# A fused token, attention and mixture-of-experts layer: the attention's normalisation on whole tiles of patches and of text

## The reference

```python
h = tok(x)                      # layernorm over 768, @ W (768x256) + bias, layernorm over 256, + position; class token first
h = concat([h, txt], axis=1)    # (16, 69, 256)
h = h + attn(layernorm(h))      # q, k, v = x @ w.T; rotary embedding; softmax(q k / 16) v, per image
h = h + ffn(layernorm(h))       # shared expert + 2 of 8 routed experts (256 -> 1024 -> 256, gelu) + x
```

## Time and profile before

| | |
|---|---|
| median of three runs | 359.08 us |
| the profiled execution, its own time | 360.22 us |
| its span, first to last instruction | 358.4 us |
| mean granted TensorE clock | 0.952 |
| TensorE busy | 309.5 us (86%) |
| GpSimd busy | 203.3 us (57%) |
| VectorE busy | 160.0 us (45%) |
| ScalarE busy | 152.5 us (43%) |

### The profile page before, as it was taken

How to read it: one execution, slowest core, us unless ns; L and a number is a source line. 1 busy time by engine, 2 the same in 40 slices (tenths; PEclk the granted TensorE clock), 3 DMA queues, 4 the chain that set the end, 5 groups by cost and what they waited for, 6 DMA issues and landing times.

```text
span 358.4 us, 6664 instructions
## 1 busy us (share of the span) xinstructions
PE 309.5 (86%) x2063; PEld 275.4 (77%) x2064; DVE 160.0 (45%) x398; ACT 152.5 (43%) x327; POOL 203.3 (57%) x155
## 2 busy tenths in 40 slices
PE   1778387899857897999989999999999999999970
PEld 1556246898737697899968998998998998998970
DVE  3244656888835264966414332332332332332320
ACT  2364431457676582435234433433433433434310
POOL 1242110843866300046598889889988889535651
PEclk9969769899985999999999999999999999999998
DMA  7934101031345433016635336523455433333522
GB/s 253 284 119 156 33 15 38 2 117 37 87 136 182 140 98 103 2 59 215 227 112 190 118 136 190 175 89 116 161 146 161 142 49 59 44 44 44 59 31 29
DMA packets 21357, 39.39 MB, mean 110 GB/s; under 512 B 2855, under 2 KB 17658, under 8 KB 19034
## 3 DMA queue, kind: packets, MB, share of 16 engines
q0 software_dynamic: 7392, 25.43, 26.5%
q1 hardware_dynamic: 13658, 13.51, 12.0%
q10 hardware_dynamic: 288, 0.20, 0.2%
HBM read 28.32 MB, written 6.93 MB: 98 GB/s over the span
## 4 chain that ended last, share of the span: by engine, by line
PE 42%; POOL 13%; DVE 12%; issue 12%; DMA 11%; ACT 3%; POOLq 3%; SPq 1%; DVEq 0%
DMA out_tokens<-xy_all,dest 10%; PE ps L898 8%; PE ps L900 8%; PE ps L899 8%; PE ps L949 7%; POOL ring L397 6%; PE ps L777 5%; PE ps L805 3%; POOL ring L396 3%; POOL out_tokens L517 2%; POOLq L514 2%; PE ps L869 2%; DVE h L1186 1%; PE ps L1012 1%; DVE st L1194 1%
## 5 line engine op out<-in xcount | busy, mean ns | idle before, releaser
L397 POOL TENSOR_TENSOR ring<-stage,ring 128x512 fp32r<-128x512 f32 (+2 forms) x30 | 76.1, 2536 | 2.5
L1439 DVE TENSOR_TENSOR hgT<-ps,hgT 128x512 fp32r<-128x512 f32 x50 | 32.2, 686 | 72.3 <-ACT hgT L767 72.3
L898 PE MATMUL ps<-ring,hgT 128*128 x200 | 58.0, 290 | 2.1 <-DVE xy_all L1445 1.5
L900 PE MATMUL ps<-ring,hgT 128*128 x200 | 55.9, 279 | 0.0
L899 PE MATMUL ps<-ring,hgT 128*128 x200 | 55.9, 279 | 0.0
L517 POOL DMA_INDIRECT out_tokens<-xy_all,dest x25 | 39.5, 1581 | 27.6 <-DMA out_tokens<-xy_all,dest 15.4
L759 ACT ACTIVATE hg<-ps 128x512 f32<-128x512 f32 x50 | 29.9, 599 | 47.7 <-PE ps L900 47.7
L507 POOL DMA_INDIRECT xy_all<-normalized_tokens,dest x25 | 24.9, 995 | 43.0 <-DVE dest L1401 35.7
L898 PE MATMUL ps<-ring,xgT 128*128 x100 | 41.3, 413 | 1.1 <-issue 0.6
L396 POOL TENSOR_SCALAR ring<-stage 128x512 fp32r<-128x512 f32 (+2 forms) x30 | 38.5, 1283 | 2.7 <-PEq L1026 2.5
L898 PEld LDWEIGHTS ps<-ring,hgT 128*128 128x128 f32 x200 | 37.6, 188 | 2.6 <-issue 2.6
(11 more groups left out here) (182 smaller groups left out, 602.2 us busy)
## 6 DMA issues: line engine op xcount, KB each, us to landing
stage<-in_w_up POOLq DMA_DIRECT2D x9, 1024.0 KB, 5.4
stage<-in_w_dn POOLq DMA_DIRECT2D x9, 1024.0 KB, 5.5
xg<-xy_all SPq DMA_DIRECT2D x25, 128.0 KB, 2.0
xp<-in_patches SPq DMA_DIRECT2D x4, 384.0 KB, 5.4
normalized_tokens<-hn SPq DMA_DIRECT2D x4, 276.0 KB
residual_tokens<-h SPq DMA_DIRECT2D x4, 276.0 KB
ring<-in_tok_w SPq DMA_DIRECT2D x1, 768.0 KB, 6.1
base<-residual_tokens SPq DMA_DIRECT2D x2, 384.0 KB, 3.6
```

The source lines that it names most:

```text
L397: return nc.gpsimd.tensor_tensor(lo, stage[:, part, c0:c1], hi.bitcast(F32), ALU.subtract)
L898: nc.tensor.matmul(o, a[0], b[0], start=n == 0, stop=False)
L900: last = nc.tensor.matmul(o, a[1], b[0], start=False, stop=n == len(pairs) - 1)
L1439: v.tensor_tensor(hgT[:, c, 1, 4 * half:4 * half + 4, :], ps[:, turned_bank + half, :].rearrange("p (k t) -> p k t", k=4), hgT[:, c, 0, 4 ...
```

## The change

1. The attention's first normalisation is made on tiles as they lie: on the five patch tiles in `tt` (which gets five buffers) and on four tiles of text rows (`xtxt`, 4 images x 32 rows each, loaded from HBM on its own). The class token is one more row (row 64) of the short tile. `attention_front`, `attention_bias`, `attention_norm` are per tile `i`, no longer per group `g`, and no longer read `h`.
2. Each of the nine tiles is transposed with two transposes. The copies out of PSUM (high on ScalarE, low on VectorE) put the columns where each image's sequence wants them, directly in `hT_n` (`placings`): one instruction for a text tile, two or three for a patch tile, since a tile cuts through images.
3. The DMAs from `tt` to `h` stay, but `h` is now first read by `attention_end`.
4. The short patch tile comes first. The text's normalisation and the high part of wq, wk, wv go to GpSimd, the position table gets `ln2_b` tile by tile, and the sum for the class token is part of `tok_end(0)`. The orders of all engines up to the first scores are rewritten.
5. `attention_qk(g)` waits for the last tile of its group (`LAST_TILE` = 1, 2, 3, 4 for the four groups).

```diff
+SHORT = NB * NPATCH % P
+TROWS = [SHORT] + [P] * (NB * NPATCH // P)
+NPT = len(TROWS)
+FIRST = [sum(TROWS[:i]) for i in range(NPT)]
...
+        def runs_of(i):
+            runs = []
+            for b, first, row, n in parts_of(i):
+                if runs and n == NPATCH and runs[-1][4] == NPATCH:
+                    runs[-1][1] += 1
+                else:
+                    runs.append([b, 1, first, row, n])
+            return runs
...
+        LAST_TILE = [max(i for i in range(NPT) if FIRST[i] < GB * NPATCH * (g + 1)) for g in range(NG)]
...
+        def placings(k, n):
+            src = turned_tile(k)
+            if k < NG:
+                return [(columns(n, GB * k, GB, 1 + NPATCH, SEQ), src.rearrange("p c (b s) -> p c b s", s=NTXT))]
+            pairs = []
+            for b, images, first, row, rows in runs_of(k - NG):
+                pairs.append((columns(n, b, images, 1 + first, 1 + first + rows),
+                              src[:, :, row:row + images * rows].rearrange("p c (b s) -> p c b s", s=rows)))
+            if k == NG:
+                pairs.append((columns(n, 0, NB, 0, 1), src[:, :, SHORT:SHORT + 1].unsqueeze(2).to_broadcast([P, KD, NB, 1])))
+            return pairs
...
+            sp.dma_start(xtxt[:, :, :], txt.rearrange("(g b) s d -> (b s) g d", g=NG)).then_inc(rows_of_text_in, 16)
             for n, v in enumerate((ln2_g, ln2_b)):
                 sp.dma_start(vecs[:, n, :], v.partition_broadcast(P)).then_inc(tok_vec_in, 16)
+            load_places(0)
             load_patches(3, NPT)
...
+            sp.dma_start(h[0:1, :, :], tt[SHORT:SHORT + 1, 0:1, :].to_broadcast([1, NB, D])).then_inc(text_in, 16)
...
+            pool.dma_start(tt[SHORT:SHORT + 1, 0, :], cls_token).then_inc(cls_in, 16)
+            pool.dma_start(pe[SHORT:SHORT + 1, 0, :], cls_pos).then_inc(cls_in, 16)
+            nc.gpsimd.memset(trs[:, :], 1.0).then_inc(ones_ready, 1)
...
+            def text_norm():
+                pool.wait_ge(x_stats, 1)
+                root(xrs[:, :], xmv[:, :, 1], P, x_rstd)
+                pool.wait_ge(x_rstd, 1)
+                for j in range(NG):
+                    nc.gpsimd.tensor_scalar(xtxt[:, j, :], xtxt[:, j, :], xmv[:, j, 0:1], xrs[:, j:j + 1], ALU.subtract,
+                                            ALU.mult).then_inc(x_normed, 1)
+
+            def place_rows_of(i):
+                pool.wait_ge(pe_in[i], 16 * (1 if i == 0 else 2))
+                r = TROWS[i]
+                nc.gpsimd.tensor_tensor(pe[0:r, i, :], pe[0:r, i, :], vecs[0:r, 1, :], ALU.add).then_inc(pe_ready, 1)
+
+            def attention_weights():
+                pool.wait_ge(attn_w_in, 48)
+                nc.gpsimd.tensor_scalar(wqk2[:, 0, :, :, :].rearrange("p w k d -> p (w k d)"),
+                                        wqk[:, :, :, :].rearrange("p w k d -> p (w k d)"), 1.0, 0.0, ALU.mult, ALU.add)
+                nc.gpsimd.tensor_scalar(wv2[:, 0, :, :].rearrange("p k d -> p (k d)"),
+                                        wvs[:, :, :].rearrange("p k d -> p (k d)"), 1.0, 0.0, ALU.mult, ALU.add).then_inc(a_whi, 1)
 
...
-            pool.wait_ge(pe_in, 16 * 9)
-            nc.gpsimd.tensor_tensor(pe[:, 0:NPT - 1, :], pe[:, 0:NPT - 1, :],
-                                    vecs[:, 1, :].unsqueeze(1).to_broadcast([P, NPT - 1, D]), ALU.add)
-            n = TROWS[NPT - 1]
-            nc.gpsimd.tensor_tensor(pe[0:n, NPT - 1, :], pe[0:n, NPT - 1, :], vecs[0:n, 1, :], ALU.add).then_inc(pe_ready, 1)
+            place_rows_of(0)
             tok_root2(0)
-            tok_root(3)
+            tok_root(4)
             load_weights(0)
+            attention_root(0)
+            place_rows_of(1)
             tok_root2(1)
-            tok_root(4)
+            attention_root(1)
+            attention_weights()
+            place_rows_of(2)
+            tok_root2(2)
             load_weights(1)
-            tok_root2(2)
-            attention_root(0)
+            attention_root(2)
+            place_rows_of(3)
             tok_root2(3)
-            attention_root(1)
+            attention_root(3)
+            place_rows_of(4)
             tok_root2(4)
+            attention_root(4)
             pool.wait_ge(a_w, 1)
             pool.wait_ge(t_mm, NPT)
-            attention_root(2)
+            pool.wait_ge(t_done, NPT)
             piece(0, 0)
             piece(0, 1)
-            attention_root(3)
...
+            def attention_copy(k):
+                act.wait_ge(a_tr, k + 1)
+                for o, i in placings(k, 0):
+                    last = nc.scalar.activation(o, i, ACT.Copy)
+                last.then_inc(a_hT, 1)
...
+            tok_turned(1)
+            tok_norm(2)
+            tok_norm(3)
+            tok_turned(2)
+            attention_copy(0)
+            attention_copy(1)
+            tok_norm(4)
             attention_norm(0)
-            tok_turned(NPT - 1)
-            attention_copy(0)
+            tok_turned(3)
+            attention_copy(2)
+            attention_copy(3)
+            attention_copy(4)
...
+            def attention_transposes(k):
+                if k < NG:
+                    te.wait_ge(x_normed, k + 1)
+                    rows = xtxt[:, k, :]
+                else:
+                    te.wait_ge(a_normed, k - NG + 1)
+                    rows = tn[0:AROWS[k - NG], k - NG, :]
+                if k >= 2:
+                    te.wait_ge(a_low, k - 1)
+                r = rows.shape[0]
+                for c in range(KD):
+                    last = transpose(turned_tile(k)[:, c, 0:r], rows[:, P * c:P * (c + 1)], r)
                 last.then_inc(a_tr, 1)
 
             def attention_qk(g):
-                te.wait_ge(a_low, g + 1)
+                te.wait_ge(a_low, NG + LAST_TILE[g] + 1)
                 if g == 0:
                     te.wait_ge(a_w, 1)
+                    te.wait_ge(t_aff, NPT)
...
+            tok_transposes(1)
+            tok_product(0)
+            tok_transposes(2)
+            attention_transposes(0)
+            attention_transposes(1)
+            tok_product(1)
+            tok_transposes(3)
+            attention_transposes(2)
+            attention_transposes(3)
+            tok_product(2)
+            attention_transposes(4)
+            tok_transposes(4)
+            tok_product(3)
+            attention_transposes(5)
+            tok_product(4)
+            attention_transposes(6)
             attention_qk(0)
...
+                r, n = AROWS[i], NPT + i
+                v.scalar_tensor_tensor(out=tt[0:r, i, :], in0=tt[0:r, i, :], scalar=trs[0:r, n:n + 1], in1=pe[0:r, i, :],
                                        op0=ALU.mult, op1=ALU.add).then_inc(t_done, 1)
...
+            def attention_front(i):
+                dve.wait_ge(t_done, i + 1)
+                r = AROWS[i]
+                link(v.bn_stats(ast[0:r, i, :], tt[0:r, i, :]))
+                link(v.bn_aggr(amv[0:r, i, :], ast[0:r, i, :]))
+                v.tensor_scalar(amv[0:r, i, 1:2], amv[0:r, i, 1:2], EPS, None, ALU.add).then_inc(a_stats, 1)
+
+            def attention_bias(i):
+                dve.wait_ge(a_rstd, i + 1)
+                r = AROWS[i]
+                v.scalar_tensor_tensor(out=anb[0:r, i:i + 1], in0=amv[0:r, i, 0:1], scalar=-1.0, in1=ars[0:r, i:i + 1],
+                                       op0=ALU.mult, op1=ALU.mult).then_inc(a_norm_in, 1)
...
+            def attention_low(k):
+                dve.wait_ge(a_hT, k + 1)
+                for (o, i), (high, _) in zip(placings(k, 1), placings(k, 0)):
+                    last = v.tensor_tensor(o, i, high.bitcast(F32), ALU.subtract)
+                last.then_inc(a_low, 1)
...
                 dve.wait_ge(a_pv, g + 1)
+                if g == 0:
+                    dve.wait_ge(text_in, 32)
+                for i in range(LAST_TILE[g - 1] + 1 if g else 0, LAST_TILE[g] + 1):
+                    dve.wait_ge(img_in[i], 16 * len(parts_of(i)))
...
+            text_stats()
+            tok_stats(3)
+            tok_shift(3)
+            tok_stats2(0)
+            tok_stats(4)
+            tok_end(0)
+            attention_front(0)
+            tok_shift(4)
+            attention_low(0)
+            attention_low(1)
+            attention_bias(0)
+            tok_stats2(1)
+            tok_end(1)
+            attention_front(1)
+            attention_low(2)
+            attention_low(3)
+            attention_bias(1)
             tok_stats2(2)
-            attention_front(0)
+            attention_weights()
+            attention_low(4)
             tok_end(2)
-            attention_bias(0)
-            attention_weights()
+            attention_front(2)
+            attention_bias(2)
             tok_stats2(3)
-            attention_front(1)
+            attention_low(5)
             tok_end(3)
-            attention_bias(1)
-            attention_low(0)
+            attention_front(3)
+            attention_bias(3)
             tok_stats2(4)
+            attention_low(6)
             tok_end(4)
```

(6 more changed lines are left out.)

200 lines of the change are left out of this document (75 added, 125 removed).

## The result

The changed kernel takes 348.69 us (median of 4 runs, 346.34 to 352.28) against 359.08: ratio 0.967, 95% interval 0.956 to 0.978. Predicted were 345.0 us and 341 to 351.5. Run again on another chip, beside 17 runs of the kernel before (median 359.28, 355.4 to 361.7), it took 349.22 us (6 runs, 347.55 to 352.62), ratio 0.976, interval 0.970 to 0.983. So it is faster by 2 to 4%, some 10 us (the second interval alone reaches down to 1.7%).

What follows compares the result with a forecast made beforehand. Start-stage stops at the class token and the DMAs into `h` were taken to bound the kernel; terms up to the probabilities summed to 14.1 us off 359.08, giving 345.0 us, with 341 to 351.5 for 8 in 10.

Steps and rivals of the forecast that it cites:

- What bounds it, and that the gain goes through: Start stages: stops at the class token's sum and 4.49 us of DMA issue into `h`; gains there move all that follows.
- To the end of the fourth tile's bias: Token stage's start: third tile's bias, text statistics, GpSimd's root and text normalisations, fourth tile's root and bias, ending at 17.4.
- GpSimd's form with two columns: Four text normalisations 128x256 on GpSimd with two columns as operands: 0.5 us each, 2.0 in all, ends 1.2 and 2.6.
- The tiles: ScalarE's turn (8.6 us), then VectorE's turns per tile, until `attention_qk(0)` starts at 41.0 in place of 52.28.
- rival 2: Small placed instructions, GpSimd's forms and contention all at upper ends: 5.6 us more, 350.5 us; chance 0.14.
- Contention: Work moved to GpSimd can stop VectorE before `attention_qk(0)`: 1.7 us taken, ends 0 and 4.3.
- the estimate by that rule: Waits for the port pair shared by GpSimd and VectorE: two of 0.3 to 0.6 and one of 1.2, 2.0 us.
- The clock ahead of the scores: `attention_qk(0)` to first scores: half clock for 3.1 us loses 1.55; 10.15 us in all, scores at 51.1.
- Scores to the shared expert: Attention loop: clock loss not paid again, shorter way to probabilities, fewer transposes; lead grows from 10.4 to 14.1 us.
- the 0.55: Net gain per group, taken twice, from groups 0 and 1 losing their eight transposes from TensorE's queue.
- From there the same distance as before: From the shared expert's first product, expected near 83, to the end: orders and distance unchanged, no more gain counted.
- Rival 1: TensorE stays at half clock in the token stage: 7 us of the gain gone, 352 us; chance 0.12.

Runs made afterwards that it cites:

- first profile: Changed kernel, no edit: profile of the slowest of its first four executions (352.28 us), span 350.4 us, clock 0.956.
- second profile: Changed kernel run again with no edit, on another chip: profile with span 345.6 us, clock 0.971; median of those runs 349.22 us.

## Why the prediction was right, step by step

- **What bounds it, and that the gain goes through.** Right in the main. The wait on `h`'s placements put back costs 23.5 us. That the class token was a stop of its own worth was only half right: alone it moves the scores by 4.65 us and the time by nothing that can be told. That TensorE is at nine tenths or more from 125 us on was read too high: the page's slices have 7 and 8 tenths from 134 to 152 us and 8 from 179 to 188.
- **To the end of the fourth tile's bias: 17.4 predicted, 21.4 and 21.8 found** (second and first profile). The term that was mis-sized is GpSimd's form with two columns: 1.21 us against 0.5, 2.8 us in all, beyond even the upper end (1.2 to 2.6 for the four, which took 4.85). The text's statistics were done 0.6 and 1.0 us later than taken, and this bias too met an add (0.5).
- **The tiles: 23.6 us from there to `attention_qk(0)` predicted, 21.1 found** (second profile; 23.0 where the clock fell early). Placed copies and low parts cost 0.46 to 0.55 us per tile on each engine, near the lower end, not 0.9 to 1.0. That is about 0.8 us on VectorE for the two tiles on this path; the rest of the 2.5 us is ticks and overlaps that the sum had counted and that I can't put to single rows. GpSimd's roots held VectorE up for 0.66 to 0.69 us three times ahead of the scores, by a hair more than the 0.6 that I had named as a sign of rival 2, without its price.
- **Contention.** 1.7 taken; five biases ahead of `attention_qk(0)` were longer by 0.5 to 0.6 each, 2.7 in all, shown for three of them by taking the adds away. A held-up bias ends when GpSimd's add does: 21.11 + 0.68 against 21.05 + 0.72. The Trainium skill ("SBUF — State Buffer", section "Who interferes with whom") says that the shared pair of ports goes to the engine that issues first, for its whole instruction, and that the other blocks. The rows agree, and the estimate by that rule, 2.0, was the nearer of the two numbers.
- **The clock ahead of the scores.** 10.15 us from `attention_qk(0)` to the scores predicted, 8.82 and 9.04 found; 7.52 and 7.51 in the two profiles with the gap filled. The loss to the clock (1.3 in the second profile) was sized rightly, the rest had 1.1 to spare. So in the second profile the scores came at 51.32 where 51.1 was predicted: 4.0 too late, then 2.5 and 1.3 too early. This near hit is luck, right by errors that cancel; in the first profile they came at 53.84.
- **Scores to the shared expert: 3.7 us shorter predicted, 2.9 found** (35.69 to 32.80 and 32.76). The first interval between scores gave 2.95 (12.63 to 9.68); the second stayed (10.68 before, 10.70 after): the transposes gone from TensorE's queue weren't alone on its path. The other path, VectorE's turn and behind it ScalarE's normalisation and its copy of the values, is as long as before (3.31 us from VectorE's `nb` to the next scores in both kernels). That is the 0.55 that failed.
- **"From there the same distance as before": failed in one profile, held in the other.** 261.2 us before, 261.5 in the second, 263.8 in the first. Between 110 and 157 us the first has stretches at 0.82 and 0.88 of full clock that the second hasn't. The same stretches below full clock stand in the profiles with the text on VectorE and with the high parts on ScalarE, so they aren't peculiar to that slowest execution. The second profile's span is 1.3 us over the predicted 344.3: 0.2 at the scores, 0.8 in the loop, 0.3 behind. Its own time, 347.55, is 1.67 below the median of its runs, where I had counted from an execution 1.14 above its median: these 2.8 us lie in which executions happened to be profiled. With 0.1 for the distance of time and span that makes the 4.2 us between 345.0 and 349.22; on the first chip it was 3.7.
- **Rival 1 (half clock in the token stage)** happened in the first profile, but VectorE waited for one product, not three: 1.9 us, not 7. The profiles of the versions with one gap filled, without the adds and with the high parts on ScalarE show it too, so the clock fell in four of the five profiles that have this 2.43 us gap. The forecast had it as the exception.

What stays open: what the new order and the short tile first are worth by themselves (with the wait on `h` in it the new order was slower than the kernel before, and without it they weren't parted); why the clock falls behind the 2.43 us gap in some executions and not in others, and what share of the median each fall has; two profiles of the kernel don't tell. The three versions with the gap filled, without the adds and with the high parts on ScalarE weren't measured beside the changed kernel, so what each is worth in time isn't known to better than 2 us.

## What to carry to other kernels

Look for a round trip through a DMA in a chain of short tiles and take it out, and check that what replaces it doesn't put a new form on GpSimd ahead of the chain's own root: a measured form on VectorE is worth more than a guess for GpSimd. When stages are shortened, look for work that is ready and stands behind another tile's round trip; here one such block, with four adds moved, brought the scores 4.6 us forward (49.41 to 44.77), 2.5 ahead of `attention_qk(0)` and 2.1 behind it, where the clock no longer fell. Before comparing two versions at the percent, put down where the clock fell in each profile, and measure them beside each other.
